# Feed-forward quarters inside self-attention given to TensorE two at a time

## The reference, cut to what matters

```python
def _attn(x, ctx, ...):            # self-attention: ctx is x; 16 heads of 32, 1024 keys
    sim = einsum('bhid,bhjd->bhij', _fq(q, dq, 128.0, 8), _fq(k, dk, 128.0, 8)) * SCALE
    attn = softmax(sim, axis=-1)
    out = einsum('bhij,bhjd->bhid', _fq(attn, dw, 0.0, 8), _fq(v, dv, 128.0, 8))
...
h3 = _ln(x, ln3_g, ln3_b)
hg = h3 @ ff_w1 + ff_b1            # 512 -> 2 x 2048
a, g = split(hg, 2, axis=-1)
x = a * gelu(g, approximate=False) @ ff_w2 + ff_b2 + x     # 2048 -> 512
```

## Time and profile before

| | |
|---|---|
| median of 3 runs | 3468.96 us (3466.39 to 3479.16) |
| the profiled execution | 3479.19 us |
| its span, first to last instruction | 3477.3 us |
| mean granted TensorE clock | 0.918 of full speed (2.4 GHz) |
| busy: VectorE, ScalarE, GpSimd | 2204.1, 1671.5, 1511.2 us |
| instructions | 50794 |
| DMA, mean over the span | 127 GB/s |

### The profile page before, as it was taken

The page is one execution under the profiler, slowest core; times in us unless marked ns, Lnnn a source line. Parts: engine busy times, 40 slices in busy tenths (PEclk is TensorE's granted clock), DMA queues, the critical chain, the costliest instruction groups (busy, mean ns, idle before and its releaser), DMA issues.

```text
span 3477.3 us, 50794 instructions
## 1 busy us (share of the span) xinstructions
PE 2963.1 (85%) x19712; PEld 2152.9 (62%) x19712; DVE 2204.1 (63%) x3543; ACT 1671.5 (48%) x2690; POOL 1511.2 (43%) x1173
## 2 busy tenths in 40 slices
PE   5468678799789889899988889889988888898999
PEld 5346545456577656656777746656777755655777
DVE  2264596786465587687565587588565588588531
ACT  4223275575333375376324276386334267277321
POOL 2364254465465154354364254354364244354221
PEclk9689856899899989899999999989999999999999
DMA  6844302234453412322453312232444322332444
GB/s 193 317 158 145 127 2 99 80 120 167 155 184 97 164 50 98 138 87 106 156 186 106 139 74 98 96 129 74 182 154 141 137 71 74 112 134 74 157 157 157
DMA packets 200621, 442.68 MB, mean 127 GB/s; under 512 B 95040, under 2 KB 103488, under 8 KB 182464
## 3 DMA queue, kind: packets, MB, share of 16 engines
q1 hardware_dynamic: 187968, 437.83, 35.1%
q10 hardware_dynamic: 12416, 1.62, 0.3%
HBM read 369.67 MB, written 65.54 MB: 125 GB/s over the span
## 4 chain that ended last, share of the span: by engine, by line
PE 53%; DVE 24%; ACT 8%; issue 5%; POOL 5%; DMA 3%; SPq 1%; ACTq 1%; POOLq 0%; DVEq 0%
PE psum L1709 16%; PE psum L1710 14%; PE psum L1711 14%; DVE mx L1589 8%; DVE w1T L1608 4%; PE psum L1998 3%; ACT e L1280 2%; PE psum L1986 2%; DVE den L1595 2%; ACT psum L1170 1%; POOL w_lo L875 1%; DVE gate L1500 1%; DMA unsplit<-in_L_xattn_ff_w 1%; PE psum L2012 1%; DMA fw_lo<-pieces 1%
## 5 line engine op out<-in xcount | busy, mean ns | idle before, releaser
L961 POOL TENSOR_SCALAR w1b<-e,rec 128x1024 f16<-128x1024 f32 x512 | 572.8, 1119 | 733.2 <-DVE rec L1597 535.0
L1589 DVE TENSOR_REDUCE mx<-psum 128x1 f32<-128x1024 f32 x512 | 622.6, 1217 | 35.0 <-PE psum L1987 34.9
L1280 ACT ACTIVATE e<-psum,nb,scale 128x1024 f32<-128x1024 f32 x512 | 617.5, 1206 | 16.8
L1709 PE MATMUL psum<-h_hi,fw_hi 128*128 128x512 f32 x1024 | 463.1, 452 | 31.3 <-DVE h_lo L1373 10.0
L1710 PE MATMUL psum<-h_lo,fw_hi 128*128 128x512 f32 x1024 | 415.5, 406 | 0.0
L1711 PE MATMUL psum<-h_hi,fw_lo 128*128 128x512 f32 x1024 | 414.2, 404 | 0.0
L1608 DVE TENSOR_SCALAR w1T<-psum 128x1024 bf16<-128x1024 f16 x512 | 348.8, 681 | 94.7 <-PE psum L1998 90.1
L1998 PE MATMUL psum<-ident,w1b 128*128 128x128 f16 x4096 | 349.4, 234 | 64.5 <-DVE w1T L1608 61.7
L1998 PEld LDWEIGHTS psum<-ident,w1b 128*128 128x128 f16 x4096 | 258.7, 104 | 233.3 <-issue 196.6
L881 POOL TENSOR_TENSOR rstd<-ve,mhalf 128x1 f32<-128x1 f32 x128 | 86.7, 678 | 497.9 <-DVE ve L1471 497.9
L1463 DVE TENSOR_TENSOR x<-psum,x 128x512 f32<-128x512 f32 x224 | 152.3, 685 | 234.8 <-PE psum L1711 234.1
(11 more groups left out here) (180 smaller groups left out, 6146.7 us busy)
## 6 DMA issues: line engine op xcount, KB each, us to landing
fw_hi<-pieces SPq DMA_DIRECT2D x168, 512.0 KB, 3.3
fw_lo<-pieces SPq DMA_DIRECT2D x168, 512.0 KB, 4.3
w_hi<-kept SPq DMA_DIRECT2D x48, 1024.0 KB, 4.9
w_lo<-kept SPq DMA_DIRECT2D x48, 1024.0 KB, 7.4
mixed<-mixed SPq DMA_DIRECT2D x32, 1024.0 KB, 4.8
fbias<-in_fside_Bx16xSxS SPq DMA_DIRECT2D x64, 256.0 KB, 2.9
unsplit<-in_L_xattn_ff_w SPq DMA_DIRECT2D x24, 512.0 KB, 5.1
pieces<-fw_hi SPq DMA_DIRECT2D x24, 512.0 KB, 2.6
```

What stands on the lines that cost most here:

```text
L961: pool.tensor_scalar(w1b[u % NH][:], e1[u % NE][:], rec1[:, u % 8:u % 8 + 1], HALF, ALU.mult, ALU.add).then_inc(w1_ready.sem, 1)
L1280: act.activation(e1[s % NE][:], psum[:, i:i + 2, :].rearrange("p i n -> p (i n)"), ACT.Exp, bias=nb1[:, s % 4:s % 4 + 1], scale=scale[:, 0:1],
L1589: dve.tensor_reduce(mx1[:, s % 4:s % 4 + 1], psum[:, i:i + 2, :].rearrange("p i n -> p (i n)"), AX, ALU.max).then_inc(maxed1.sem, 1)
L1709: pe.matmul(o, s_hi, m_hi, start=first, stop=False)
```

## The change

The number of quarters given by the end of a slot of self-attention was the share 4 x in_S x (s+1) / 70, rounded down to a whole quarter. It is now that share rounded down to two quarters (half a step, 6 matmuls). Nothing else is edited.

```diff
     first, start = 4 * NC * in_A, len(ends)
     for s in range(S_SLOTS):
-        ends.append(min(first + 4 * in_S, first + 4 * in_S * (s + 1) // (S_SLOTS - 1)))
+        ends.append(min(first + 4 * in_S, first + 2 * (2 * in_S * (s + 1) // (S_SLOTS - 1))))
     for s in range(M_SLOTS):
```

## The result

| | before | changed |
|---|---|---|
| median | 3472.03 us (4 runs, 3466.39 to 3479.16) | 3503.20 us (4 runs, 3498.46 to 3506.25) |
| ratio | | 1.0088, 95% interval 1.0068 to 1.0108 |
| the profiled execution | 3479.19 us | 3498.46 us |
| its span | 3477.3 us | 3496.6 us |
| mean granted clock | 0.918 | 0.920 |

The change makes the kernel 0.9% slower, 31 us in the medians. So each term is read stage by stage, not from the spans.

What follows compares the result with a forecast made beforehand. VectorE was taken to bound the 18-step stages and TensorE the 28-step ones. Losses of 15.4 us (28 steps) and 18.9 us (18 steps) sum to +34.3 us on 3468.96, so 3503 us, range 3472 to 3530.

Steps and rivals of the forecast that it cites:

- Only TensorE's order changes, steps end in the same slots.: All touched stages: only TensorE's quarters move, 214 by one slot; other engines' programs stay, no instruction added or removed.
- Empty slots, 28 steps, 3.9 us a stage.: 28-step stages: TensorE waits 5.4 us at the transposes' bank, less 1.5 for openings; 15.4 us for four stages.
- The two waits, 0.62 and 0.28 us: Empty slots of 28-step stages: transposes wait for w1T 0.62 us, or 0.28 with weighted sums before; six of each.
- Nothing later gives this back: 28-step stages: the waits in empty slots are not recovered later, because TensorE is the bound.
- Joined openings, 0.11 us each.: A quarter joined to another saves 0.11 us: 1.5 us per 28-step stage, taken as 0 in 18-step stages.
- Double slots, 18 steps, 6.3 us a stage.: 18-step stages: double slots bring VectorE's transposes late, 3.6 + 2.7 us a stage, 18.9 us for three.
- the 0.30 for every pair of slots 10 to 33: 18-step stages: loss taken for each of 12 slot pairs, between 0.21 (loop mean) and 0.46 (transposes' lateness); 3.6 us.
- the 0.38 of the loop through the bank: 18-step stages: with weighted sums the loop takes 4.21 us against VectorE's 3.83; seven pairs from slot 36, 2.7 us.
- VectorE's own feed-forward work falls in the pairs without weighted sums and hides nothing of this: 18-step stages: VectorE's feed-forward instructions, 0.685 us each in one slot of four, do not absorb the double slots' loss.
- The sign named for this term: 18-step stages: w1T's wait for the transposes was to grow by some 6 us, all along the stage.
- The median would be +34.3 us.: Whole kernel: 15.4 us from 28-step and 18.9 us from 18-step stages, added to 3468.96 us, give 3503 us.
- Rival 3, the clock.: Touched stages: one in ten of 448 slots falls to half clock, 48 us more, 3551 us; chance 6%.

Runs made afterwards that it cites:

- The placement pair: Two kernels, against the one before: only 28-step stages hand out halves, with 15 empty slots after weighted sums (3478.53 us) or not after sums (3497.56 us).
- even double slots: Against the kernel before, only 18-step stages hand out halves, with double slots in the even slots throughout: 3491.35 us, ratio 1.0057; a second time 3482.80 us.
- whole steps: Against the kernel before, quarters are handed out four at a time in all seven stages: 3695.41 us beside 3470.61, one execution.

## Why the prediction was right

The forecast, 3503 us and slower, is what was measured, and its direction and its main mechanism hold: TensorE waits at the bank where a slot has no quarter. Its terms did not all have the right size, and the exact hit is partly luck.

- *Only TensorE's order changes, steps end in the same slots.* Right: 50794 instructions in both, and VectorE's and ScalarE's busy times in the stages are equal within 0.7 us.
- *Empty slots, 28 steps, 3.9 us a stage.* Measured: 3.4, 3.0, 3.1 and 2.9 us in numbers 1, 3, 5 and 7, 12.5 in all where 15.4 had been put, and 3.3 us in number 5 with this kind alone. Of the 3.4 us in number 1 an unknown part is the clock's. The two waits, 0.62 and 0.28 us, are in the timeline to 0.01 us, and the total at the bank rose by 5.1 us (2.9 to 8.0) against 5.4 worked out. The placement pair shows by experiment that the place of the empty slots matters, though at full clock by less than the waits say. "Nothing later gives this back" was not quite right: the scores' wait for the exponential fell by 0.9 us in number 5 (10.8 to 9.9), which is about what the term was too large by.
- *Joined openings, 0.11 us each.* Seen in the double slot's 1.51 us (2312.23 to 2313.74). That they are hidden in the 18-step stages was taken, and no run shows it by itself.
- *Double slots, 18 steps, 6.3 us a stage.* Too large by a factor of two: numbers 2, 4 and 6 grew by 3.0, 2.6 and 3.9 us, 9.4 in all where 18.9 had been put. Number 4 at full clock says the same: slots 16 to 32 grew by 1.0 us where eight pairs at 0.30 make 2.4, and slots 40 to 60 by 0.9 where five pairs at 0.38 make 1.9. Two steps failed. The first is the 0.30 for every pair of slots 10 to 33. Taken from the start of a maximum to that of two slots later, the four pairs with weighted sums in slots 16 to 32 grew by 0.32 to 0.43 us, which is the 0.38 of the loop through the bank. The four without got shorter by 0.1 us in the mean (0.26 shorter to 0.07 longer), and a lateness of 0.46 in every pair is not there. They had taken 3.83 to 4.71 us before, and the prediction read 3.83 from one pair as VectorE's pace for all. The second is "VectorE's own feed-forward work falls in the pairs without weighted sums and hides nothing of this". That is so in slots 16 to 32. From slot 40 on it is wrong: before the change each of the five pairs with sums (slots 42, 46, 50, 54, 58) holds one such instruction of 0.68 or 0.74 us on VectorE. Two of them, in slots 43 and 51:

```profile
2107.28 0.68 DVE L1463 TENSOR_TENSOR x<-psum,x 128x512 f32<-128x512 f32 x1
...
2123.73 0.74 DVE L1500 SCALAR_TENSOR_TENSOR gate<-psum,col_L_xattn_ff_b,gate 128x512 f32<-128x512 f32 x1
```

  The pairs of slots 46 and 50 grew by 0.4 us and those of 42, 54 and 58 by under 0.1. Why two of the five pay and three do not stays open. The sign named for this term, w1T waiting 6 us more for the transposes, also missed: 3.8 to 5.2 us. The loop shows at its other end, the transposes at the bank (6.6 to 18.1 us).
- *The median would be +34.3 us.* It is +31, but the stages give 21.9. The transposes and sums left after the last maximum give more: the first matmul of the next projection (`w_hi` by `ht_hi`) starts 16.62 us after the end of the last maximum in number 7 (15.94 before) and 14.05 in number 4 (13.13 before): 4 x 0.7 + 3 x 0.9 = 5.5 us, which the prediction had left out. 27 us are thus located, inside the ratio's interval (24 to 37 us). The remaining 4 us are not located: the two profiled executions lie 19 us apart, so the rest of the kernel took 8 us less in the changed one, against the 12 us by which the two stand off their medians. The near hit of 3503 is partly luck: one term too large, one left out.
- *Rival 3, the clock.* Not in the changed kernel. In its two profiles the clocks of stages 1 to 7 lie between 0.92 and 0.95, as before (0.92 to 0.96). It is real nearby, as the runs show.

## What to carry to other kernels

A small piece of work between two dependent pieces on one engine is a cover, and its worth is read from the round trip of the buffer that the second piece needs, here 1.49 us from one start of the transposes to the next. Hand such work out evenly, at least one piece to every slot, before thinking of longer groups: the 0.11 us saved by an opening stood against 0.28 to 0.62 us of waiting. If gaps can't be avoided, put them where other work of the same engine lies next to them; and look at the clock of the stages, since a regular gap may cost more through it than by itself. Before one variant is called better by 1 or 2 us in a stage, compare stretches with the same clock: here 2 of 3.0 us of a hit that had been forecast lay where the clocks differed.

## What the runs showed of the hardware that was not expected

**The clock can swing in steady turns.** In self-attention 6 of the run with even double slots the granted clock alternates. The table by stretch shows four stretches in turn, then 61 us of self-attention 4 of the same execution:

```profile
2892.50:2895.50 3.00, 3.00 (x18) 2.00 (x16) 1.86 (x4) 2.83 (x6) 0.11 (x1) 0.50 0.02 5
2896.00:2902.50 6.50, 5.13 (x56) 3.25 (x57) 6.41 (x11) 3.67 (x8) 3.85 (x4) 1.00 0.00 0
2903.00:2905.50 2.50, 2.50 (x13) 1.68 (x11) 1.03 (x3) 2.20 (x5) 0.00 (x0) 0.50 0.00 0
2906.00:2912.50 6.50, 5.15 (x63) 3.21 (x56) 6.34 (x10) 3.50 (x8) 3.78 (x4) 1.00 0.82 318
2085.30:2146.30 61.00, 51.73 (x589) 34.00 (x588) 59.03 (x93) 47.03 (x90) 34.62 (x32) 0.99 0.17 61
```

At 1.2 GHz (0.50) TensorE is busy all the time; at 2.4 GHz (1.00) it is busy 5.13 of 6.50 us, with the waits of the empty slots in between, and the clock falls again. Each turn lasts 10.2 us, four slots that take 8.7 us elsewhere. From slot 41 to the end the clock falls six times, 3.4 us each, nine times in the whole stage against two and three in numbers 2 and 4. In self-attention 4 the same program at the same places keeps 0.99. The Trainium skill, page "TensorE: Matmul & The Clock Gate", section "A second HAM failure mode: psum-queue depth-cycling", tells of such a swing through short idle times between groups of matmuls. The runs agree with it for even double slots (0.87 against 0.97) and for whole steps (0.78), and disagree for the changed kernel, whose transposes wait for the bank nearly as long (18.1 us in self-attention 4, against 19.8 with even double slots at 0.97) and whose clock stays. What decides between them stays open.

**A group's opening depends on what is ahead of it.** A quarter costs 0.70 us behind another quarter, 0.81 behind the scores and 0.88 behind the transposes (0.90 behind the weighted sums, in the run with the second quarter behind them), all at full clock.
